# DLRM tower on one core: padded tables for ten one-hot picks, and ids laid out per partition

## The reference, cut to what matters

```python
e = jnp.stack([tbl_0[ids[:, 0]], tbl_1[ids[:, 1]], ..., tbl_25[ids[:, 25]]], axis=1)   # (512, 26, 128)
combined = jnp.concatenate([dense[:, None, :], e], axis=1)                              # (512, 27, 128)
inter = jnp.einsum('bnd,bmd->bnm', combined, combined)[:, triu_i, triu_j]               # 351 pairs
h = jnp.concatenate([dense, inter, dense], axis=1)                                      # (512, 607)
h = jnp.maximum(h @ W_top1 + b_top1, 0.0)                                               # 512
h = jnp.maximum(h @ W_top2 + b_top2, 0.0)                                               # 256
y = h @ W_top3
```

## Time and profile before

| what | us |
|---|---|
| median of 3 runs | 178.63 (176.61 to 180.29) |
| span of the profiled execution | 175.4 |
| TensorE matmul busy | 101.8 (58%) |
| TensorE weight load busy | 87.2 (50%) |
| VectorE busy | 59.5 (34%) |
| ScalarE busy | 64.1 (37%) |
| GpSimd busy | 74.0 (42%) |

### The profile page before, as it was taken

How to read it: one execution, slowest core, us unless ns; L and a number is a source line. 1 busy time by engine, 2 the same in 40 slices (tenths; PEclk the granted TensorE clock), 3 DMA queues, 4 the chain that set the end, 5 groups by cost and what they waited for, 6 DMA issues and landing times.

```text
span 175.4 us, 3474 instructions
## 1 busy us (share of the span) xinstructions
PE 101.8 (58%) x1500; PEld 87.2 (50%) x1500; DVE 59.5 (34%) x140; ACT 64.1 (37%) x126; POOL 74.0 (42%) x80
## 2 busy tenths in 40 slices
PE   0049630029910562211039985599978997997894
PEld 0037410017800450110028764599867996996793
DVE  2636200538001700000098621273147035534501
ACT  2064810049001700000299394173336235444420
POOL 1087777777777777772637777100000000000000
PEclk9999995555996566555556999789999999999999
DMA  3334444444431142111017983100000000000000
GB/s 75 131 139 163 151 168 155 159 153 152 151 122 49 46 152 65 59 46 30 30 32 211 262 272 98 32 4 0 4 4 4 0 4 4 4 0 4 4 0 0
DMA packets 5910, 13.75 MB, mean 78 GB/s; under 512 B 2216, under 2 KB 3240, under 8 KB 5643
## 3 DMA queue, kind: packets, MB, share of 16 engines
q1 hardware_dynamic: 3064, 8.77, 14.8%
q0 software_dynamic: 2304, 4.72, 9.1%
q10 hardware_dynamic: 528, 0.05, 0.3%
HBM read 13.54 MB, written 0.00 MB: 77 GB/s over the span
## 4 chain that ended last, share of the span: by engine, by line
PE 32%; another core or an unknown queue 22%; DMA 21%; DVE 13%; issue 7%; SPq 2%; ACT 2%
DMA ids_row<-ids_picked 16%; PE dots_ps L480 11%; PE acc_ps L506 11%; DVE onehot L370 6%; DMA table_raw<-tbl 5%; PE h_ps L521 4%; DVE table_lo L376 3%; PE turn_ps L460 3%; DVE z L264 2%; SPq L195 2%; PE acc_ps L439 1%; PE acc_ps L445 1%; ACT cols L282 1%; DVE z L257 1%
## 5 line engine op out<-in xcount | busy, mean ns | idle before, releaser
L236 POOL DMA_INDIRECT rows<-tbl,ids_sb x72 | 73.1, 1016 | 35.4 <-issue 21.0
L439 PE MATMUL acc_ps<-onehot,table_hi 125*128 125x512 f32 x64 | 23.3, 523 | 38.4 <-DVE onehot L370 20.9
L370 DVE TENSOR_SCALAR onehot<-ids_row,row_number 125x512 fp32r<-125x512 int32 x56 | 23.0, 481 | 57.0 <-remote 39.5
L439 PEld LDWEIGHTS acc_ps<-onehot,table_hi 125*128 125x128 f32 x64 | 15.8, 257 | 45.3 <-issue 38.7
L445 PE MATMUL acc_ps<-onehot,table_lo 125*128 125x512 f32 x64 | 19.8, 439 | 12.1 <-issue 12.1
L282 ACT ACTIVATE cols<-turn_ps 128x512 f32<-128x512 f32 (+1 forms) x16 | 15.3, 970 | 30.3 <-remote 25.1
L480 PE MATMUL dots_ps<-cols 128*32 128x26 f32 x1024 | 19.9, 197 | 7.9 <-issue 7.1
L480 PEld LDWEIGHTS dots_ps<-cols 128*32 128x32 f32 x1024 | 18.7, 118 | 9.6 <-issue 8.2
L445 PEld LDWEIGHTS acc_ps<-onehot,table_lo 125*128 125x128 f32 x64 | 13.4, 217 | 15.3 <-issue 12.8
L282 ACT ACTIVATE z<-dots_ps 25x160 f32<-25x160 f32 (+4 forms) x56 | 13.7, 258 | 17.5 <-PE dots_ps L480 16.9
L506 PE MATMUL acc_ps<-z,w_sb 128*128 128x128 f32 x160 | 18.8, 277 | 1.3 <-DVE z L264 1.3
(11 more groups left out here) (26 smaller groups left out, 43.8 us busy)
## 6 DMA issues: line engine op xcount, KB each, us to landing
table_raw<-tbl SPq DMA_DIRECT2D x8, 500.0 KB
w_sb<-w SPq DMA_DIRECT2D x1, 1792.0 KB
ids_row<-ids_picked SPq DMA_DIRECT2D x1, 1500.0 KB
rows<-tbl,ids_sb POOLq DMA_INDIRECT x72
w_sb<-w SPq DMA_DIRECT2D x1, 512.0 KB
ids_row<-ids_picked SPq DMA_DIRECT2D x2, 250.0 KB
dense_sb<-dense SPq DMA_DIRECT2D x1, 256.0 KB, 9.5
ids_sb<-ids ACTq DMA_DIRECT2D x1, 52.0 KB, 7.8
```

The lines of the kernel that those rows point to most:

```text
L236: nc.gpsimd.indirect_dma_start(rows[:, t % GATHER_RING, n, :], None, tables[f][:, :], index).then_inc(rows_in[t][g], 16)
L370: nc.vector.tensor_scalar(onehot[:, k % 2, c, :], ids_row[:, k, :], row_number[0:PICK_PARTS, c:c + 1], None, ALU.is_equal).then_inc(onehot ...
L439: nc.tensor.matmul(acc_ps[k % 2][:], table_hi[:, k % 2, c, :], onehot[:, k % 2, c, :], start=(c == 0), stop=False)
```

## The change

The number of picked tables goes from 8 to 10, and that of gathered tables from 18 to 16: `NG` becomes 4, and every group has four tables. The ten picked tables are padded with zero rows on the host from 1,000 to 1,024 rows and given as one tensor, so that each is loaded as 128 partitions x 8 rows (512 KB). All tiles and matmuls of the picks have 128 partitions in place of 125, the broadcast ids too. The third load of broadcast ids has eight tables. The ids for the gathers are laid out by the host as partition, tile, table, so that their load is one run of 416 bytes per partition. `early_groups(0)` is 3 (it would be 4, but the last group is turned elsewhere).

```diff
-PICK_PARTS = 125
+PICK_PARTS = P
 PICK_ROWS = 8
+PICK_TABLE_ROWS = 1000
 ACT_CHUNKS = 1
-NUM_PICKED = 8
-PICKED = [f for f, rows in enumerate(TABLE_ROWS) if rows == PICK_PARTS * PICK_ROWS][:NUM_PICKED]
+NUM_PICKED = 10
+PICKED = [f for f, rows in enumerate(TABLE_ROWS) if rows == PICK_TABLE_ROWS][:NUM_PICKED]
...
 def early_groups(t):
-    return EARLY_GROUPS + (FIRST_GROUPS if t == 0 else 0)
+    return min(EARLY_GROUPS + (FIRST_GROUPS if t == 0 else 0), NG - 1)
...
             def load_table(k):
-                src = tables[PICKED[k]].rearrange("(p c) d -> p c d", c=PICK_ROWS)
+                src = picked_tables[k].rearrange("(p c) d -> p c d", c=PICK_ROWS)
                 sp.dma_start(table_raw[:, k % 2], src).then_inc(table_in[k % 2], 16)
...
-            act.dma_start(ids_sb[:], ids.rearrange("(t p) f -> p t f", p=P)).then_inc(ids_in, 16)
+            act.dma_start(ids_sb[:], ids).then_inc(ids_in, 16)
...
     ids = np.asarray(inputs["ids"])
+    padded = np.zeros((NUM_PICKED, PICK_PARTS * PICK_ROWS, DIM), w.dtype)
+    for k, f in enumerate(PICKED):
+        padded[k, :PICK_TABLE_ROWS] = inputs[f"tbl_{f}"]
...
-          declare("ids", ids),
+          declare("ids", ids.reshape(TILES, P, NUM_TABLES).transpose(1, 0, 2)),
           declare("ids_picked", ids[:, PICKED].T),
-          [declare(f"tbl_{f}", inputs[f"tbl_{f}"]) for f in range(NUM_TABLES)],
+          declare("picked_tables", padded),
+          {f: declare(f"tbl_{f}", inputs[f"tbl_{f}"]) for f in GATHERED},
```

More of the change, by code:

```diff
@@ L101, in moved_count, with build @@
                if (t, g) <= (tile, group))
-def build(nc, dense, ids, ids_picked, tables, w1, w2, w3, b1, b2, out):
+def build(nc, dense, ids, ids_picked, picked_tables, tables, w1, w2, w3, b1, b2, out):
     with ExitStack() as ctx:
```

## The result

The kernel after takes 172.25 us (median of 4 runs, 171.39 to 173.38), the kernel before 177.78 us beside it (4 runs, 176.61 to 180.29). The ratio is 0.968, 95% interval [0.960, 0.977]: faster, by 6 us where I had forecast 28. The result is outside my range of 122 to 160. So there are two results, and the explanation has to hold for both.

What follows compares the result with a forecast made beforehand. It took idle waits in the picks, from slow loads and the crawl, as the bound, not the tail. Gathers' end 91.5 + tail 63.5 + 0.9 - 7 progress = 149 span, plus 1.5: 150 us, range 122 to 160.

Steps and rivals of the forecast that it cites:

- likeliest case: Tile 0's dots: TensorE stays slow until the last gather, then the tail follows; 150 us, 142 to 157, chance 0.42.
- rival 1: Tile 0's dots: no crawl once loads are fast; span 122.7, time 125 us, 118 to 131, chance 0.30.
- crawl: TensorE completing very slowly while gathers run beside no bulk load, seen in picks and tile 0's dots; 2.8 us per matmul.
- Loads: Tables and ids for the picks: 200 GB/s in place of 107, 2.6 us a table; ids 2 to 9 in by 21 us.
- Start of the dots: Tile 0, after ten picks with a period of 4.7 us: dots can start at 57.5 us, bounds 51 and 63.
- Gathers: GpSimd: 64 gathers at 1.31 us each from 6 us on, the last issued at 90 us.
- The end of the crawl: Tile 0's dots: last gather landed and its effect gone at 91.5 us, 1.5 us after its issue.
- Progress in the crawl: Tile 0's dots, 57.5 to 91.5 us: about 280 matmuls done slowly, worth 7 us at normal pace.
- Tail: From the crawl's end to the end of the kernel: 63.5 us as before, plus 0.9 for three tiles' copies.
- Partial crawl: Some stretches of the picks or tile 0 slow, but not until the last gather; 131 to 142 us, chance 0.20.
- rival 3: The crawl takes the picks that turn tile 0, delaying tile 3's gathers; 167, or 182 or more, chance 0.05.
- Rival 4: Loads of the picks do not speed up; two more tables and their ids add 14.4 us; about 184, chance 0.03.

Runs made afterwards that it cites:

- h1: Kernel after, unaltered, run once more in a job where the kernel before took 139.24 us: 122.46 us, ratio 0.885.
- e5: Kernel after with eight extra 128x1024 subtractions on VectorE before its first move behind tile 0's dots: 163.81 us, ratio 0.921.
- e3: Kernel after with TensorE waiting, before tile 1's first turn and tile 0's dots, until all gathers of tile 3 have landed: 171.58 us.
- e11: Kernel after with eight picked tables in place of ten, so only the padding and the ids' layout remain: 175.26 us, ratio 0.984.
- h2: Kernel before with ten picked tables in place of eight, unpadded, ids as before: 157.13 us, ratio 1.132.
- e8: Kernel after with a GpSimd memset of 768 columns as a pause behind each gather of tiles 2 and 3: 141.1 us, ratio 0.793.
- g4: Kernel after with GpSimd memsets of 768 columns as pauses behind the gathers of tiles 1 to 3: 144.19 us, ratio 1.035.
- e10: Kernel after with a GpSimd memset of 256 columns as a pause behind each gather of tiles 2 and 3: 171.0 us, ratio 0.960.
- e12: Kernel before with GpSimd memsets of 768 columns as pauses behind each gather of tiles 1 to 3: 155.64 us, ratio 0.874.

## Why the prediction was wrong

**Which kernel is meant.** My likeliest case and rival 1 are two states of the same kernel, and I had taken them for two theories of which one had to fall. Rival 1 said a span of 122.7 and 125 us; h1 has a span of 120.7 and 122.46 us (picks 5 us shorter, tail 3 us longer than its sum). That the two misses cancel is luck, and its reason was wrong: the fast loads do not end the crawl, since the kernel after has them and crawls. For the result on record the case I put first is the right one: TensorE crawls until the last gather, and the tail follows. What failed is the sum behind it, by 171.6 - 149 = 22.6 us of span, in three terms and a rest, all taken too small: the end of the gathers (8.7 us), the progress credited to the crawl (6.4), the recovery (5.1) and the tail (2.6).

**Loads: right, and faster than taken.** 260 to 296 GB/s in the windows for my 200, with the gathers' 52 among them. After pick 2 no table is waited for by more than 0.21 us. The ids of picks 2 to 9 ended the wait at 15.76, not 21.

**Start of the dots: 52.35 for 57.5**, inside my 51 to 63. The "half clock" that I gave the first pick is in no row: the granted clock of the kernel before is 1.00 from 11 to 18 us, though the first high part takes 3.76 us and later ones 2.11. The first pick took about as long after (3.64 us for the high part), so the term held. The period of a pick is (43.64 - 9.38) / 8 = 4.3 us for my 4.7, with the wait of 2.29 in it, and 4.0 without: ScalarE's turn copies do not stretch it.

**Gathers: the first term mis-sized.** I took 1.31 us each from the mean of before. After, they are (97.72 - 4.98) / 63 = 1.47 us apart, and the last ends at 98.67, not at 90. The step that failed is "one costs 1.31 us": the mean of before holds a long stretch in which VectorE stood still and a gather took 0.94 plus 0.30 us. Beside the busy picks of the kernel after a gather takes 0.94 to 3.60, and the first 26 are 1.81 us apart on average; behind the picks they are 1.25 apart. The row at 55.94 in e5 shows such a slow gather, 1.96 us, beside subtractions of 128x1024. The Trainium skill (SBUF — State Buffer, section "Who interferes with whom") says that VectorE and GpSimd share a pair of ports as an exclusive lock, so that descriptors of GpSimd's DMAs wait for some VectorE operations. It also says that a probe saw no DMA stalled by `tensor_tensor`; e5's filler is such an operation and its gathers take 0.98 to 1.96 us, so here the measurement decides. That section was there to be weighed against this term.

**The end of the crawl: 105.23 for 91.5.** Of the 13.73 us, 8.67 are the gathers (98.67 for 90) and 5.06 the recovery of 6.56 us, which I had at 1.5 from before.

**Progress in the crawl: the term read worst.** "At the pace of 32 dots in 3.9 us" I credited all of tile 0's dots and 2 us more, 7 us. But 27 of these 32 ran in the first 0.60 us, and the other 5 took 3.3 us; and the pace falls to one matmul in 2.8 us, as the earlier trace rows already showed. 90 of 256 dots were done in 53 us, and the other 166 took 4.45 us, at a granted clock of 0.50, against 5.06 for 224: 0.6 us won, not 7. e3 prices it independently: without the stretch, the same time.

**Tail:** 66.4 us measured; 64.4 less the 0.6 is 63.8, so 2.6 us are left over. "issue" pieces of 1.1 to 1.5 us in the later dots make 5.3 us, for 3.4 before, which covers 1.8 of them; the rest I cannot place. Such pieces stand in h1 too, so they are not the crawl. And "gathers as data are hidden" failed in h1, by the 0.79 us that TensorE waits for them. 13.7 + 6.4 + 2.6 = 22.7: the error is placed, but for this rest.

**Why only 6 us.** The crawl lasts until the last gather. Before, it is issued at 109.18, after at 97.72, 11.5 us earlier. Of these, 4.9 went into the longer recovery (6.6 for 1.7) and 2.9 into a longer tail (66.4 for 63.5). That leaves 3.8, the two spans' difference (175.4 less 171.6). The faster picks, 55 us earlier at the dots (107.98 and 52.35), are invisible: they freed TensorE for a time in which it could not work. The gain was real (h1), and turned into a new wait.

**Rivals 2, 3 and 4.** Partial crawl: did not come. The crawl did not reach the picks in the kernel after, but does in e11, so rival 3 names a real mechanism, with eight picked tables. Rival 4 (no faster loads) fell with the loads; its price for two tables and their ids over slow loads, 14.4 us, is near the 18 us that h2 costs.

## What to carry to other kernels

Before you credit a faster stage, ask what the engine would do with the time, and look in the trace for a stretch in which it has work and does not do it ("issue" between single instructions); what ends that stretch is the bound, and here it was the last indirect gather of another engine. If such a stretch exists, take its price at its slowest rows, not at its first ones, and look whether the engine that ends it will be slowed by the very stage that you make faster. And have the kernel before run beside every comparison: here one and the same kernel took 139 or 178 us, and pauses that were worth 31 us in the one case (e8) cost 22 in the other (g4, from one tile earlier on).

## What the runs showed of the hardware

- **Indirect gathers from GpSimd, back to back, can all but stop TensorE.** For matmuls of 26 columns, in the jobs with the crawl: 1.25 us apart, in the end one matmul in 2.8 us; 1.44 apart, some 3 per gather (e10); 1.87 apart, 50 per gather (e8); 2.27 apart for three gathers, with VectorE busy beside them, full pace (e5). Picks of 512 columns beside a busy VectorE ran at full pace at 1.38. Plain loads from the same queue and bulk traffic at 273 GB/s do neither harm nor good. The granted clock is not the cause: in the kernel after, the first gaps of 1.18 us stand at 53 to 56 us, where it is still 1.00 (2.4 GHz); it is 0.50 (1.2 GHz) from 56 to 60 us, after TensorE was busy 0.36 of the 2 us before. The Trainium skill (SBUF — State Buffer, section "Who interferes with whom") says that only that one pair of ports causes contention; TensorE is not on it, and the runs show it held up all the same, so the measurement decides. The physical cause is open. One candidate that no run tested is the supply of instructions: from 52 us to the end of the gathers the queue of instruction fetches moved one packet (0.02 MB) in the kernel after and eight (0.13 MB) in h1, which can be the cause of the crawl or only its trace.
- **It comes and goes with the job.** Every job up to e12 had it (before 177 to 179 us), the last two had none (139 us). Jobs of both kinds ran on a chip of the same number. What decides stays open; that the kernel before crawled in none of the last two jobs is read from its time, not from a trace of it.
- **A memset on GpSimd between gathers doubles VectorE's one-hots beside it**: seven took 2.86 us without pauses and 6.07 to 6.43 beside them, in e12 and g4. The first slow one in g4's timeline of VectorE:

```profile
31.87 6.11 DVE L379 TENSOR_SCALAR onehot<-ids_row,row_number 128x512 fp32r<-128x512 int32 x7
```

- **128 partitions in place of 125** moved the loads from about 107 GB/s beside the gathers to 210 to 240 (260 and 296 less the gathers' 52), and the DMA share from 0.45 to 0.75 to 0.80. The absence of the crawl does not do it: h2, ten tables of 125 partitions with no crawl, has 0.45 at 163 GB/s between 30 and 35 us. The Trainium skill's rule (DMA: Bandwidth & Descriptors, section "Why a DMA increments its semaphore by 16 and not by 1"), 5 engines for 125 partitions and 16 for 128, fits these shares; no view counts the engines.
